# Attention on one core: which engine makes the low halves of the split scores

## The chip, the cores and the metric

The kernel runs on one core of one Trainium2 chip. The metric is the device time in microseconds (us) of one launch. Five engines work side by side and meet at semaphores: TensorE (PE in the profile, its weight loads PEld), VectorE (DVE), ScalarE (ACT), GpSimd (POOL) and SyncE (SP), which issues most of the DMAs.

## What is computed

Three layers follow each other over 16 sequences of 512 tokens with 256 features. The change lies in the second, a causal linear attention with 16 heads of 64. Cut to its core:

```python
h = _ln(x, g1, beta1)
q = _phi((h @ wq).reshape(b, s, H, DH), proj)      # phi(x) = elu(x @ proj) + 1
k = _phi((h @ wk).reshape(b, s, H, DH), proj)
v = (h @ wv).reshape(b, s, H, DH)
def step(carry, qkv_t):
    kv, ksum = carry
    kv = kv + k_t[..., :, None] * v_t[..., None, :]
    ksum = ksum + k_t
    num = jnp.einsum('bhd,bhde->bhe', q_t, kv)
    den = jnp.einsum('bhd,bhd->bh', q_t, ksum) + 1e-06
    return ((kv, ksum), num / den[..., None])
attn = moveaxis(outs) @ wo
x = x + attn
```

An MLP and a routed expert layer come behind it.

## The kernel before

The scan over tokens is done in four chunks of 128 tokens per sequence (CH = 4). Within a chunk TensorE makes the scores of key and query features, VectorE masks them, and TensorE multiplies them with the values; what lies before the chunk comes in through running sums of key times value (kvacc). All products run in float16: each operand is split into a high half (a cast) and a low half (what the cast lost), and three matmuls (high by high, low by high, high by low) give one product (the function `three`).

The 16 heads of a chunk are taken in two ways. The scores come in four quads q = 0 to 3, each a tile of 128 x 512: `scores` on TensorE writes pS, VectorE masks it into sm (L902), ScalarE casts sm to the high half sh (L796), and one engine subtracts to get the low half sl. The outputs come in four groups g = 0 to 3. Groups 0 and 1 read quads 0 and 1, groups 2 and 3 read quads 2 and 3, so `outputs` on TensorE waits for two quads when g is even (L667 to L669). Before, GpSimd makes the low halves of quads 0 and 2 (L978) and VectorE those of quads 1 and 3 (L909).

The order on every engine is written out by hand, by one function `run` that every engine walks through with its own steps. Half a sequence, a unit, is eight slots s = 0 to 7: slot s belongs to chunk 2h + s // 4 and group g = s % 4, where h is the half. In a slot an engine does, in this order: the early dense work of the table DENSE (features of the next unit "f", values "v", the projection "p"), `outputs` of this slot's group, the transposes of an earlier group, the read-out of the early dense work, `scores` of the quad that this slot brings in, `outputs_split` (on, oh, ol), the late dense work, `sums` (kvacc), `keys` (kt), `scores_split` (sh, sl), `sums_split` (kvh, kvl), a part of the split and the mixing of the input three units ahead (xh, xl), and the read-out of the late dense work (z, hi, lo). The quad of a slot runs two slots ahead of its use: slots g = 0 and 1 bring quads 2 and 3 of their own chunk, slots g = 2 and 3 bring quads 0 and 1 of the next chunk. Quad 1 is thus the last thing made before group 0 of the next chunk wants it.

I number the chunks of a sequence 1 to 4. "The outputs of chunk 2" means its group 0, which opens slot 4 of the first half, right behind slot 3, the slot of the values v0 and v1.

sm has two buffers, one for even and one for odd quads. ks, qdh and qdl (keys and queries) reach their place by DMAs of SyncE, which wait for hi and lo.

Of the kernel before, what the change touches and what calls it, by code (L numbers as in the profile page):

```python
# [10 lines left out]
ALU = mybir.AluOpType  # L11
# [13 lines left out]
CH = 4  # L25
# [29 lines left out]
def count(i, per, k):  # L55

    return i * per + k


def units(u, per, k):  # L60

    return count(u[0], 2 * per, u[1] * per + k)
# [7 lines left out]
def some(value):  # L70

    return type(value) is not int or value > 0
# [22 lines left out]
def attention_phase(nc, io, w1_w, w2_w, mlp_loaded):  # L95
# [4 lines left out]
    with ExitStack() as ctx:  # L100
        def sb(name, shape, dt=F32):
            return ctx.enter_context(nc.sbuf_tensor(name, [P, *shape], dt))

        def sem(name):
            return ctx.enter_context(nc.semaphore(name))
# [147 lines left out]
        sm = sb("sm", [2, 4, P])  # L253
        sh, sl = sb("sh", [4, 4, P], F16), sb("sl", [4, 4, P], F16)
# [22 lines left out]
            sem("qk_done"), sem("e_ready"), sem("z_read"), sem("f_ready"), sem("fh_ready"), sem("fl_ready"))  # L277
        v_done, vh_ready, vl_ready, v_ones = sem("v_done"), sem("vh_ready"), sem("vl_ready"), sem("v_ones")
        s_done, sm_ready, sh_ready = sem("s_done"), sem("sm_ready"), sem("sh_ready")
        sl_ready = [sem("sl_even"), sem("sl_odd")]  # L280
        o_done, dn_ready, rd_ready, on_ready, oh_ready, ol_ready = (
            sem("o_done"), sem("dn_ready"), sem("rd_ready"), sem("on_ready"), sem("oh_ready"), sem("ol_ready"))
        turned, turn_read = sem("turned"), sem("turn_read")
# [8 lines left out]
        def place(u):  # L292

            return (2 * u[0] + u[1]) % AHEAD
# [9 lines left out]
        def move_done(engine, w, n):  # L304


            kind = n % MOVES // 2
            engine.wait_ge(moved[kind], (128, 64)[kind] * (units(w, FEATS // MOVES, n // MOVES) + 1))
# [6 lines left out]
        def feature_back(w, n):  # L315
            return (w, n - MOVES) if n >= MOVES else (after(w, -1), n - MOVES + FEATS)

        def score_place(h):
            return 2 * (h // 8) + h % 2, (h % 8) // 2
# [227 lines left out]
        def _(pe):  # L547
            def three(out, wh, wl, mh, ml, first, last):

                pe.matmul(out, wh, mh, start=first, stop=False, skip_group_check=True)  # L550
                pe.matmul(out, wl, mh, start=False, stop=False, skip_group_check=True)  # L551
                return pe.matmul(out, wh, ml, start=False, stop=last, skip_group_check=True)  # L552
# [95 lines left out]
            def outputs(i, c, g):  # L648
                n = 4 * c + g
                toks = slice(c * P, (c + 1) * P)  # L650
                out = pO[g % 2]

                if some(count(i, 16, n - 1)):
                    pe.wait_ge(on_ready, count(i, 16, n - 1))
                first = True
                if c > 0:
                    pe.wait_ge(kvh_ready, count(i, NKV, 4 * (c - 1) + g + 1))
                    pe.wait_ge(kvl_ready, count(i, NKV, 4 * (c - 1) + g + 1))
                    for k in range(4):
                        h, part = 4 * g + k, out[:, VW * k:VW * (k + 1)]  # L660
                        pe.matmul(part, qdh[:, h, toks], kvh[:, h, :], start=first, stop=False, skip_group_check=True)
                        first = False
                        pe.matmul(part, qdh[:, h, toks], kvl[:, h, :], start=False, stop=False, skip_group_check=True)
                        pe.matmul(part, qdl[:, h, toks], kvh[:, h, :], start=False, stop=False, skip_group_check=True)
                if g % 2 == 0:

                    pe.wait_ge(sh_ready, count(i, 16, 4 * c + g + 2))  # L667
                    pe.wait_ge(sl_ready[0], count(i, 8, 2 * c + g // 2 + 1))
                    pe.wait_ge(sl_ready[1], count(i, 8, 2 * c + g // 2 + 1))  # L669
                if g == 0:  # L670
                    if type(i) is int and i == 0 and c == 0:
                        pe.wait_ge(v_ones, 2)
                    pe.wait_ge(vh_ready, count(i, 2 * VALS, 2 * c + 2))
                    pe.wait_ge(vl_ready, count(i, 2 * VALS, 2 * c + 2))
                for k in range(4):
                    h = 4 * g + k
                    q, w = score_place(h)
                    mm = three(out[:, VW * k:VW * (k + 1)], sh[:, q, w, :], sl[:, q, w, :],
                               vh[:, c, h, :], vl[:, c, h, :], first, True)
                    first = False  # L680
                mm.then_inc(o_done, 1)
# [13 lines left out]
            def turn(i, c, g):  # L695
# [6 lines left out]
                for part, src in enumerate((oh, ol)):  # L702
                    for f in range(2):
# [3 lines left out]

            run(pe, dict(mix=mix, mean=mean, var=var, features=features, values=values, scores=scores, keys=keys,
                         outputs=outputs, sums=sums, turn=turn, project=project))

        @block.scalar
# [123 lines left out]
        def _(ve):  # L835
# [60 lines left out]
            def scores(i, c, q):  # L896
                n = 4 * c + q
                ve.wait_ge(s_done, count(i, 16, n + 1))
                if some(count(i, 16, n - 1)):
                    ve.wait_ge(sh_ready, count(i, 16, n - 1))  # L900
                    ve.wait_ge(sl_ready[q % 2], count(i, 8, 2 * c + q // 2))
                nc.vector.tensor_tensor(sm[:, n % 2, :, :], pS[:, :].rearrange("p (a b) -> p a b", b=P),  # L902
                                        mask[:, :].unsqueeze(1).broadcast_to([P, 4, P]),
                                        ALU.mult).then_inc(sm_ready, 1)

            def scores_split(i, c, q):
                if q % 2 == 1:
                    ve.wait_ge(sh_ready, count(i, 16, 4 * c + q + 1))
                    nc.vector.tensor_tensor(sl[:, q, :, :], sm[:, 1, :, :], sh[:, q, :, :],  # L909
                                            ALU.subtract).then_inc(sl_ready[1], 1)  # L910

            def keys(i, c, part):
                ve.wait_ge(turned, key_turn(i, c, part))
# [43 lines left out]
        @block.gpsimd  # L957
        def _(gp):
            gp.memset(vh[:, :, :, DH:VW], 1.0).then_inc(v_ones, 1)
            gp.memset(vl[:, :, :, DH:VW], 0.0).then_inc(v_ones, 1)  # L960

            def split(u, k):
                gp.wait_ge(xh_ready, units(u, XS, k + 1))
                if some(units(u, XS, k + 1 - XS)):
                    gp.wait_ge(tok_done, units(u, XS, k + 1 - XS))
                nc.gpsimd.tensor_tensor(xl[:, k, :, :], xs[:, k, :, :], xh[:, k, :, :], ALU.subtract).then_inc(xl_ready, 1)  # L966

            def phi(w, n, bank_no):
                if units(w, FEATS, n) >= MOVES:
                    move_done(gp, *feature_back(w, n))  # L970
                gp.wait_ge(fh_ready, units(w, FEATS, n + 1))
                nc.gpsimd.tensor_tensor(lo[n % MOVES // 2][:, n % 2, :, :], z[:, units(w, FEATS, n) % ZS, :, :], hi[:, n % MOVES, :, :],  # L972
                                        ALU.subtract).then_inc(fl_ready, 1)

            def scores_split(i, c, q):
                if q % 2 == 0:
                    gp.wait_ge(sh_ready, count(i, 16, 4 * c + q + 1))
                    nc.gpsimd.tensor_tensor(sl[:, q, :, :], sm[:, 0, :, :], sh[:, q, :, :],  # L978
                                            ALU.subtract).then_inc(sl_ready[0], 1)

            def outputs_split(i, c, g):
                n = 4 * c + g
                gp.wait_ge(oh_ready, count(i, 16, n + 1))
                nc.gpsimd.tensor_tensor(ol[:, n % 2, :], on[:, n % 2, :, :].rearrange("p a b -> p (a b)"),  # L984
                                        oh[:, n % 2, :], ALU.subtract).then_inc(ol_ready, 1)

            def sums_split(i, c, g):
                u = 4 * c + g
                gp.wait_ge(kvh_ready, count(i, NKV, u + 1))
                heads = slice(4 * g, 4 * g + 4)  # L990
                nc.gpsimd.tensor_tensor(kvl[:, heads, :], kvacc[:, heads, :], kvh[:, heads, :],  # L991
                                        ALU.subtract).then_inc(kvl_ready, 1)

            def residual(u):
                gp.wait_ge(x1_ready, units(u, 1, 1))
                gp.wait_ge(h_ready, units(u, 1, 1))
                gp.wait_ge(hb_ready, units(u, DT, DT))
                nc.gpsimd.tensor_tensor(hT[:, place(u), :, :], hT[:, place(u), :, :], x0[:, place(u), :, :],
                                        ALU.add).then_inc(hx_ready, 1)

            run(gp, dict(residual=residual, split=split, phi=phi, scores_split=scores_split, outputs_split=outputs_split,
                         sums_split=sums_split))

# [1194 lines left out]
```

## Time and profile before

| what | value |
|---|---|
| median of 3 runs | 2622.9 us (2621.56 to 2630.17) |
| profiled execution, its time | 2629.9 us |
| profiled execution, its span | 2628.2 us |
| PE busy | 2258.0 us, 86% |
| DVE busy | 1783.4 us, 68% |
| ACT busy | 1525.8 us, 58% |
| POOL busy | 1468.2 us, 56% |
| attention, from its first outputs to its last | about 113 to 1525 us of the span |

Busy time is a share of the whole span, in which three stages follow each other; only the attention stage holds the instructions that the change moves. One sequence takes 90 us there. A busy PE is one whose matmul records overlap, so a stall shows as an idle time in front of a matmul, in square brackets in the timeline.

### The profile page before, as it was taken

The page shows a single profiled execution, that of the slowest core. Times are in us where ns is not written, and L with a number is a line of the kernel's source. Part 1 is how long each engine was busy: PE and PEld are TensorE (multiplying, and loading weights), DVE is VectorE, ACT ScalarE, POOL GpSimd, SP SyncE. Part 2 cuts the span into 40 slices and gives each one's busy share as a digit, 9 for nine tenths or more (in the row PEclk, how much of TensorE's full clock was granted, in tenths as well). Part 3 has the DMA queues.
Part 4 walks back from the last instruction along what each step waited for, and adds up shares of the span by engine and source line. Part 5 has one row for each costly group of instructions (what it writes and reads, how often), then busy time and mean ns, then how long its engine had stood idle before and what let it go on. Part 6 is the DMA issues. An engine that isn't in the chain of part 4 may idle for free. (4 is left out here: it accounts for less than half of the span.)

```text
span 2628.2 us, 64033 instructions
## 1 busy us (share of the span) xinstructions
PE 2258.0 (86%) x24112; PEld 1738.2 (66%) x24112; DVE 1783.4 (68%) x3983; ACT 1525.8 (58%) x2890; POOL 1468.2 (56%) x1449
## 2 busy tenths in 40 slices
PE   3799999999999999999999858989998999894774
PEld 2588787878787887878787736555555555552553
DVE  2477778777777777777777746766776677664442
ACT  3576777767777777677677645544554455441232
POOL 1376666666666756666666621553454345436576
PEclk8899999999999999999999979999999999997887
DMA  3344444444444434444443330111111111000775
GB/s 109 101 129 126 108 123 128 123 117 123 125 116 123 115 97 114 100 105 105 114 102 90 82 107 33 57 52 54 42 57 66 40 35 46 27 21 17 156 141 71
DMA packets 310913, 236.32 MB, mean 90 GB/s; under 512 B 28057, under 2 KB 275853, under 8 KB 310608
## 3 DMA queue, kind: packets, MB, share of 16 engines
q1 hardware_dynamic: 274352, 197.25, 28.1%
q0 software_dynamic: 23808, 21.74, 4.7%
q10 hardware_dynamic: 12448, 13.24, 1.6%
q8 instruction: 194, 3.18, 0.5%
q14 instruction: 111, 0.91, 0.1%
HBM read 73.32 MB, written 82.58 MB: 59 GB/s over the span
## 5 line engine op out<-in xcount | busy, mean ns | idle before, releaser
L1857 POOL DMA_INDIRECT slot_dram<-xt,slot_u x256 | 267.4, 1045 | 77.1 <-issue 77.1
L550 PE MATMUL pF<-nh,qk_h 128*128 128x256 f16 x1024 | 281.7, 275 | 7.8 <-DVE nl L869 4.4
L551 PE MATMUL pF<-nh,qk_l 128*128 128x256 f16 x1024 | 281.5, 275 | 0.0
L552 PE MATMUL pF<-nl,qk_h 128*128 128x256 f16 x1024 | 281.3, 275 | 0.0
L972 POOL TENSOR_TENSOR lo<-z,hi 128x512 f16<-128x512 f32 x128 | 148.6, 1161 | 198.6 <-DVE hi L881 198.6
L1845 POOL TENSOR_TENSOR xt<-xn,xt 128x512 f16<-128x512 f32 x32 | 40.0, 1269 | 330.5 <-ACT xt L1528 330.5
L796 ACT ACTIVATE sh<-sm 128x512 f16<-128x512 f32 x256 | 160.0, 625 | 88.2 <-DVE sm L902 82.5
L984 POOL TENSOR_TENSOR ol<-on,oh 128x256 f16<-128x256 f32 x256 | 172.2, 673 | 69.5 <-ACT oh L819 69.5
L876 DVE SCALAR_TENSOR_TENSOR z<-pF,z 128x512 f32<-128x512 f32 x256 | 175.1, 684 | 41.6 <-ACT z L779 39.0
L972 POOL TENSOR_TENSOR w_w<-z,hi 128x512 f16<-128x512 f32 x128 | 157.7, 1232 | 60.4 <-DVE hi L881 60.4
L991 POOL TENSOR_TENSOR kvl<-kvacc,kvh 128x260 f16<-128x260 f32 x192 | 157.9, 822 | 50.3 <-ACT kvh L827 50.3
L902 DVE TENSOR_TENSOR sm<-pS,mask 128x512 f32<-128x512 f32 x256 | 174.4, 681 | 10.1 <-PE pS L636 10.1
L1309 PE MATMUL pY<-w_h,gh 128*128 128x256 f16 x512 | 154.5, 302 | 30.0 <-issue 29.8
L550 PE MATMUL pO<-vh,sh 128*128 128x65 f16 x1024 | 119.4, 193 | 67.7 <-issue 48.1
L881 DVE CAST hi<-z 128x512 f16<-128x512 f32 x256 | 170.5, 666 | 8.8
L775 ACT ACTIVATE z<-pF 128x512 f32<-128x512 f32 x256 | 149.9, 586 | 45.1 <-PE pF L552 42.9
L966 POOL TENSOR_TENSOR xl<-w_w,xh 128x512 f16<-128x512 f32 x128 | 148.0, 1159 | 47.3 <-ACT xh L726 47.3
L1311 PE MATMUL pY<-w_l,gh 128*128 128x256 f16 x512 | 154.1, 301 | 22.4 <-issue 22.0
L1310 PE MATMUL pY<-w_h,gl 128*128 128x256 f16 x512 | 154.6, 302 | 18.6 <-issue 18.4
L803 ACT ACTIVATE ot<-pT 128x512 f16<-128x512 f16 x256 | 149.8, 585 | 31.0 <-PE pT L705 30.3
L779 ACT ACTIVATE z<-z 128x512 f32<-128x512 f32 x256 | 161.3, 630 | 8.2
L2107 POOL DMA_INDIRECT out_rows<-yb,xg x80 | 126.7, 1584 | 61.4 <-ACT yb L2052 35.9
(299 smaller groups left out, 8517.1 us busy)
## 6 DMA issues: line engine op xcount, KB each, us to landing
w_w<-in_x SPq DMA_DIRECT2D x128, 256.0 KB, 3.0
qdh<-hi SPq DMA_DIRECT2D x256, 128.0 KB, 2.7
qdl<-lo SPq DMA_DIRECT2D x256, 128.0 KB, 2.8
ks<-hi SPq DMA_DIRECT2D x128, 128.0 KB, 3.1
ks<-w_w SPq DMA_DIRECT2D x128, 128.0 KB, 3.1
slot_dram<-blank ACTq DMA_DIRECT2D x8, 1360.0 KB, 6.7
xg<-slot_dram SPq DMA_DIRECT2D x40, 272.0 KB, 2.9
x_dram<-x SPq DMA_DIRECT2D x32, 256.0 KB, 2.2
```

The lines of the kernel that those rows point to most:

```text
L550: pe.matmul(out, wh, mh, start=first, stop=False, skip_group_check=True)
L551: pe.matmul(out, wl, mh, start=False, stop=False, skip_group_check=True)
L552: return pe.matmul(out, wh, ml, start=False, stop=last, skip_group_check=True)
L779: nc.scalar.activation(z[:, s, :, :], z[:, s, :, :], ACT.Exp, scale=-1.0, bias=-math.log(PHI_DOWN)).then_inc(e_ready, 1)
L796: nc.scalar.activation(sh[:, q, :, :], sm[:, n % 2, :, :], ACT.Copy).then_inc(sh_ready, 1)
L876: nc.vector.scalar_tensor_tensor(z[:, s, :, :], pF[bank_no][:, :].rearrange("p (b n) -> p b n", b=2), 0.0, z[:, s, :, :], ALU.max, ALU.add ...
L881: nc.vector.tensor_copy(hi[:, n % MOVES, :, :], z[:, s, :, :]).then_inc(fh_ready, 1)
L902: nc.vector.tensor_tensor(sm[:, n % 2, :, :], pS[:, :].rearrange("p (a b) -> p a b", b=P), mask[:, :].unsqueeze(1).broadcast_to([P, 4, P]) ...
L972: nc.gpsimd.tensor_tensor(lo[n % MOVES // 2][:, n % 2, :, :], z[:, units(w, FEATS, n) % ZS, :, :], hi[:, n % MOVES, :, :], ALU.subtract).t ...
L984: nc.gpsimd.tensor_tensor(ol[:, n % 2, :], on[:, n % 2, :, :].rearrange("p a b -> p (a b)"), oh[:, n % 2, :], ALU.subtract).then_inc(ol_re ...
L991: nc.gpsimd.tensor_tensor(kvl[:, heads, :], kvacc[:, heads, :], kvh[:, heads, :], ALU.subtract).then_inc(kvl_ready, 1)
L1857: nc.gpsimd.indirect_dma_start(io["slot_dram"], bass.IndirectOffsetOnAxis(slot_u[:, i % XT, c, k:k + 1], 0), xt[:, i % XT, c, :], None, bo ...
```

## The change

The low halves of quads 0 and 1 change engines: GpSimd now makes those of quads 1 and 2, VectorE those of quads 0 and 3. Each engine still makes two of four. The semaphore that counted the low halves by parity becomes one for each quad, and every wait keeps its meaning. In the slots this means that the subtraction of slots 2 and 6 (quad 0) moves from GpSimd to VectorE and that of slots 3 and 7 (quad 1) from VectorE to GpSimd.

```diff
-        sl_ready = [sem("sl_even"), sem("sl_odd")]
+        sl_ready = [sem(f"sl_ready{q}") for q in range(4)]
...
-                    pe.wait_ge(sl_ready[0], count(i, 8, 2 * c + g // 2 + 1))
-                    pe.wait_ge(sl_ready[1], count(i, 8, 2 * c + g // 2 + 1))
+                    pe.wait_ge(sl_ready[g], count(i, CH, c + 1))
+                    pe.wait_ge(sl_ready[g + 1], count(i, CH, c + 1))
...
-                    ve.wait_ge(sl_ready[q % 2], count(i, 8, 2 * c + q // 2))
+                    ve.wait_ge(sl_ready[(q + 2) % 4], count(i, CH, c + q // 2))
...
             def scores_split(i, c, q):
-                if q % 2 == 1:
+                if q in (0, 3):
                     ve.wait_ge(sh_ready, count(i, 16, 4 * c + q + 1))
-                    nc.vector.tensor_tensor(sl[:, q, :, :], sm[:, 1, :, :], sh[:, q, :, :],
-                                            ALU.subtract).then_inc(sl_ready[1], 1)
+                    nc.vector.tensor_tensor(sl[:, q, :, :], sm[:, q % 2, :, :], sh[:, q, :, :],
+                                            ALU.subtract).then_inc(sl_ready[q], 1)
...
             def scores_split(i, c, q):
-                if q % 2 == 0:
+                if q in (1, 2):
                     gp.wait_ge(sh_ready, count(i, 16, 4 * c + q + 1))
-                    nc.gpsimd.tensor_tensor(sl[:, q, :, :], sm[:, 0, :, :], sh[:, q, :, :],
-                                            ALU.subtract).then_inc(sl_ready[0], 1)
+                    nc.gpsimd.tensor_tensor(sl[:, q, :, :], sm[:, q % 2, :, :], sh[:, q, :, :],
+                                            ALU.subtract).then_inc(sl_ready[q], 1)
```

On VectorE, in slots 2 and 3 of the first half, from the transposed keys kt of slot 2 to the first instruction of the outputs of chunk 2 (dn), the order before is:

```order
L917 COPY kt<-pT 128x1024
L876 SCALAR_TENSOR_TENSOR z<-pF,z 128x512
L881 CAST hi<-z 128x512
L886 SCALAR_TENSOR_TENSOR vl<-pF,vh 128x8x64
L926 TENSOR_SCALAR dn<-pO 128x4
L929 RECIPROCAL rd<-dn 128x4
L934 TENSOR_TENSOR on<-pO,rd 128x256
L902 TENSOR_TENSOR sm<-pS,mask 128x512
L886 SCALAR_TENSOR_TENSOR vl<-pF,vh 128x8x64
L947 COPY kvacc<-pKV 128x260
L909 TENSOR_TENSOR sl<-sm,sh 128x512
L926 TENSOR_SCALAR dn<-pO 128x4
```

The same stretch of VectorE with the change:

```order
L917 COPY kt<-pT 128x1024
L909 TENSOR_TENSOR sl<-sm,sh 128x512
L876 SCALAR_TENSOR_TENSOR z<-pF,z 128x512
L881 CAST hi<-z 128x512
L886 SCALAR_TENSOR_TENSOR vl<-pF,vh 128x8x64
L926 TENSOR_SCALAR dn<-pO 128x4
L929 RECIPROCAL rd<-dn 128x4
L934 TENSOR_TENSOR on<-pO,rd 128x256
L902 TENSOR_TENSOR sm<-pS,mask 128x512
L886 SCALAR_TENSOR_TENSOR vl<-pF,vh 128x8x64
L947 COPY kvacc<-pKV 128x260
L926 TENSOR_SCALAR dn<-pO 128x4
```

The subtraction stood last, behind the mask of quad 1 (sm) that it needs; now one stands ahead of z, and the mask of quad 1 comes after it. On GpSimd, in the same two slots, from the residual (hT) of slot 2 to the input split (xl) of slot 3, the order before is:

```order
L998 TENSOR_TENSOR hT<-hT,x 128x512
L984 TENSOR_TENSOR ol<-on,oh 128x256
L978 TENSOR_TENSOR sl<-sm,sh 128x512
L991 TENSOR_TENSOR kvl<-kvacc,kvh 128x260
L966 TENSOR_TENSOR xl<-w_w,xh 128x512
L972 TENSOR_TENSOR w_w<-z,hi 128x512
L984 TENSOR_TENSOR ol<-on,oh 128x256
L991 TENSOR_TENSOR kvl<-kvacc,kvh 128x260
L966 TENSOR_TENSOR xl<-w_w,xh 128x512
```

And with the change (w_w at L972 is the low half of key features, lo):

```order
L998 TENSOR_TENSOR hT<-hT,x 128x512
L984 TENSOR_TENSOR ol<-on,oh 128x256
L991 TENSOR_TENSOR kvl<-kvacc,kvh 128x260
L966 TENSOR_TENSOR xl<-w_w,xh 128x512
L972 TENSOR_TENSOR w_w<-z,hi 128x512
L984 TENSOR_TENSOR ol<-on,oh 128x256
L978 TENSOR_TENSOR sl<-sm,sh 128x512
L991 TENSOR_TENSOR kvl<-kvacc,kvh 128x260
L966 TENSOR_TENSOR xl<-w_w,xh 128x512
```

GpSimd's subtraction moves five places back, behind the ol of slot 3. TensorE, ScalarE and SyncE keep their order.

## Rows read from the trace of the kernel before

**Rows 1.** Windows, most of the attention stage: length, busy time and instructions by engine, PEclk, DMA

```profile
150.00:1450.00 1300.00, 1213.44 (x16192) 1040.27 (x16190) 1004.52 (x2081) 922.77 (x1875) 851.32 (x893) 1.00 0.44 114
```

**Rows 2.** Waits of PE from 150 to 1450: us in total, times, longest

```profile
PE pO L550 <- issue: 44.5, 29, 1.8
PE pT L645 <- ACT ot L803: 31.2, 28, 1.5
PE pO L550 <- DVE sl L909: 8.9, 28, 0.7
```

**Rows 3.** Timeline, chunk 1 of a sequence: start, length, instruction, idle before it

```profile
1011.11 0.42 ACT L819 ACTIVATE oh<-on 128x256 f16<-128x256 f32 x1 [0.55 <-DVE on L934]
...
1011.60 0.68 POOL L984 TENSOR_TENSOR ol<-on,oh 128x256 f16<-128x256 f32 x1 [1.97 <-ACT oh L819]
...
1011.70 0.63 ACT L796 ACTIVATE sh<-sm 128x512 f16<-128x512 f32 x1 [0.18 <-DVE sm L902]
...
1012.36 0.69 DVE L909 TENSOR_TENSOR sl<-sm,sh 128x512 f16<-128x512 f32 x1 [0.70 <-ACT sh L796]
...
1013.42 0.19 PE L550 MATMUL pO<-vh,sh 128*128 128x65 f16 x1 [0.43 <-DVE sl L909]
```

**Rows 4.** Timeline, chunk 2: PE, its features f4 and its outputs

```profile
1034.31 0.28 PE L550 MATMUL pF<-nh,qk_h 128*128 128x256 f16 x1
...
1037.97 0.19 PE L550 MATMUL pO<-vh,sh 128*128 128x65 f16 x1 [1.81 <-issue]
```

**Rows 5.** Timeline, slots 2 and 3 ahead of chunk 2: DVE

```profile
1031.12 0.68 DVE L917 COPY kt<-pT 128x1024 f16<-128x1024 f16 x1
...
1032.43 1.23 DVE L881 CAST hi<-z 128x512 f16<-128x512 f32 x1
1033.57 0.68 DVE L886 SCALAR_TENSOR_TENSOR vl<-pF,vh 128x512 f16<-128x512 f32 x1
...
1036.90 0.68 DVE L909 TENSOR_TENSOR sl<-sm,sh 128x512 f16<-128x512 f32 x1
```

**Rows 6.** Timeline, chunk 3: DVE's subtraction, and the outputs on PE

```profile
1057.43 0.69 DVE L909 TENSOR_TENSOR sl<-sm,sh 128x512 f16<-128x512 f32 x1 [0.36 <-ACT sh L796]
...
1058.50 0.19 PE L550 MATMUL pO<-vh,sh 128*128 128x65 f16 x1
```

**Rows 7.** Timeline, slots 2 and 3 again: POOL, and ACT's cast of quad 1

```profile
1031.58 0.68 POOL L984 TENSOR_TENSOR ol<-on,oh 128x256 f16<-128x256 f32 x1
1032.21 1.16 POOL L978 TENSOR_TENSOR sl<-sm,sh 128x512 f16<-128x512 f32 x1
...
1034.15 1.15 POOL L966 TENSOR_TENSOR xl<-w_w,xh 128x512 f16<-128x512 f32 x1
...
1035.83 0.62 ACT L796 ACTIVATE sh<-sm 128x512 f16<-128x512 f32 x1
```

**Rows 8.** Timeline, DVE and POOL in each other's way, and a cast left alone

```profile
1002.51 0.67 POOL L984 TENSOR_TENSOR ol<-on,oh 128x256 f16<-128x256 f32 x1
1003.13 1.13 POOL L991 TENSOR_TENSOR kvl<-kvacc,kvh 128x260 f16<-128x260 f32 x1
...
1002.54 1.18 DVE L909 TENSOR_TENSOR sl<-sm,sh 128x512 f16<-128x512 f32 x1 [0.36 <-ACT sh L796]
...
1004.36 0.43 DVE L881 CAST hi<-z 128x512 f16<-128x512 f32 x1
```

**Rows 9.** Timeline, the end of the stage: PE released by POOL

```profile
1514.47 0.69 POOL L991 TENSOR_TENSOR kvl<-kvacc,kvh 128x260 f16<-128x260 f32 x1
...
1515.31 0.19 PE L661 MATMUL pO<-kvh,qdh 128*128 128x65 f16 x1 [1.21 <-POOL kvl L991]
```

**Rows 10.** Timeline, slot 7 of the second half: DVE waits for the values

```profile
1009.64 0.69 DVE L886 SCALAR_TENSOR_TENSOR vl<-pF,vh 128x512 f16<-128x512 f32 x1 [1.84 <-ACT vh L785]
```

**Rows 11.** Timeline, in the opening of the stage: a long wait of PE

```profile
85.20 1.40 PE L579 MATMUL pM<-w_w,ones 128*128 128x256 f32 x4 [2.93 <-ACT w_w L737]
```

**Rows 12.** Windows, behind that wait, columns as in rows 1

```profile
85.90:89.30 3.40, 3.40 (x16) 2.22 (x16) 1.15 (x3) 2.05 (x5) 0.00 (x0) 0.50 0.00 0
```

## The prediction

> **What bounds the kernel now.** I read the windows first: over 1300 us of attention PE is busy 1213, VectorE 1005, ScalarE 923, GpSimd 851 [rows 1]. TensorE bounds the stage, and only what makes it stand still counts. The waits of PE say where that is: 85 us in all, and 53 of them stand in front of the first matmul that uses sh and sl, pO at L550 [rows 2]. So the change touches the largest stall there is. 44.5 us of it carry the label "issue", which names nobody, so I went to the timeline. In each sequence there are four such places, the outputs of chunks 1 to 4, and they differ.
>
> Chunk 1: the high half of quad 1 ends at 1012.33, VectorE's subtraction runs 1012.36 to 1013.05, TensorE starts at 1013.42 after 0.43 us idle [rows 3]. The subtraction is the last link. Chunk 2: the subtraction ends at 1037.58 and TensorE starts 0.39 later, having stood for 1.81 [rows 4, 5]; the 29 "issue" waits, two in each sequence, have a mean of 44.5 / 29 = 1.53 [rows 2], so chunks 2 and 4 are alike: the subtraction releases TensorE there too. Chunk 3: it ends at 1058.12, TensorE comes at 1058.50 without idle time [rows 6]. In chunk 1 TensorE needed 0.37 from that end, where a bare wait takes 0.06 [rows 4, 5], so its slack here lies between 0 and 0.32; I take 0.17, the middle.
>
> In slots 2 and 3 ahead of chunk 2 VectorE is the one who is late: its cast hi takes 1.23 instead of 0.43, because GpSimd's sl runs from 1032.21 to 1033.37, and the cast ends 0.29 behind it [rows 5, 7, 8].
>
> **The change part by part.** Each engine keeps two of four subtractions, so busy times hardly move. What moves is who stands last, and what is in front.
>
> *Quad 1 from VectorE to GpSimd, all four places.* GpSimd takes 1.16 [rows 7] where VectorE takes 0.69: +0.47. It starts 0.07 to 0.08 behind ScalarE (oh ends at 1011.53, ol starts at 1011.60 [rows 3]), VectorE 0.03: +0.05. Its queue is clear: ol ends at 1012.28, before sh does [rows 3]. TensorE starts 0.15 behind the end of a GpSimd instruction (1515.16 to 1515.31 [rows 9]); behind VectorE it takes 0.06 where one wait is all (vl ends 1034.25, f4 starts 1034.31 [rows 4, 5]): +0.09. Together 0.61. Chunk 1 pays all of it. Chunk 3 pays 0.61 - 0.17 = 0.44.
>
> *Quad 0 from GpSimd to VectorE, slots 6.* VectorE then waits for the values v3, 1.84 us [rows 10]. A subtraction of 0.7 to 1.2 fits under this wait: nothing. If that cover were gone, it would cost these.
>
> *Quad 0 from GpSimd to VectorE, slots 2.* Here VectorE has no gap. kt ends at 1031.80 [rows 5], the high half of quad 0 is ready then, and sl would start at 1031.82. But GpSimd's ol runs until 1032.26 [rows 7]. The same pair meets in another slot [rows 8]: VectorE's sl begins 0.03 behind the start of ol, lasts 1.18 instead of 0.69 and ends 0.54 behind the end of ol, and GpSimd's next, kvl, ends 0.54 behind sl instead of taking its usual 0.68. So sl ends near 1032.80, a full microsecond behind kt. The cast starts 0.63 behind the end of what stands ahead of z (kt 1031.80, hi 1032.43 [rows 5]): 1033.43. GpSimd now has kvl, then xl: kvl ends at 1033.34, xl starts 0.04 before that, at 1033.30, and takes 1.15 [rows 7], to 1034.45. The cast comes 0.13 too late, waits, and ends 0.29 behind xl at 1034.74, against 1033.66 now. So v0's low half, on, oh, the mask of quad 1 and its high half all come 1.08 later; VectorE works through them without a pause worth counting. GpSimd has caught up by then (lo, then ol, end before sh, at 1036.45 + 1.08 = 1037.53 [rows 7]).
>
> From the end of sh to the end of sl it is now 1037.58 - 1036.45 = 1.13, as kvacc stands in the way; on GpSimd 0.08 + 1.16 = 1.24: +0.11. With the reaction of 0.09 and the 1.08 this is 1.28 in chunk 2, and the same in chunk 4, whose slots hold the same instructions. I take the whole 1.08 because both meetings are of a kind that the trace shows. Its ends are 0.22 if the cast gets in ahead of xl, when GpSimd's delayed queue makes the sum some 0.41; and some 1.5 if GpSimd's next instruction also got in ahead of sl. Part of this stall shows earlier: f4 waits for v0's low half and starts 0.06 behind it [rows 4, 5], so about 1 us of idle time appears in front of pF.
>
> *Sum.* 0.61 + 1.28 + 0.44 + 1.28 = 3.61 us for a sequence. The first and the last sequence lack a part, so 15.5 of them: **+56 us**. The profiled time is 2629.9, within 0.3% of the median of 2622.9; the same increment on the median gives **2679**. The delays are not made good elsewhere, since all the chains behind start from TensorE.
>
> The Trainium skill (GPSIMD Engine Reference, Instruction dispatch) puts the floor of a two-input GpSimd operation at about 2.5 cycles per element. At its 1.2 GHz that is an estimate of 1.07 us for 512 elements; with it the four places would cost 0.36 less in a sequence, and the sum would be some 50 us. The rows have 1.16, and I go by them.
>
> **The rivals.** *The cast is not caught (0.12).* The margin is 0.13 us, the difference of sums over several rows. If hi starts before xl, chunks 2 and 4 pay 0.41 each: 0.61 + 0.44 + 0.82 = 1.87, times 15.5 is 29, so 2652. For it: the margin is small. Against it: nothing in front of xl waits. The Trainium skill (SBUF — State Buffer, Who interferes with whom) says that the first of the two to start holds the shared ports for its whole instruction, the other blocks; by that rule the cast loses, with xl started 0.13 before it.
>
> *The clock (0.06).* In the opening TensorE stood 2.93 us [rows 11], and from 85.90 to 89.30 its granted clock was 0.50, the lower level of 1.2 GHz [rows 12]; in attention it is 1.00 with stalls up to 1.81 [rows 1, 4]. The longer stall is parted by f4 into about 1.0 and 1.75, so I expect no fall. If each of 31 places fell for 3.4 us, half of that is lost: 31 x 1.7 = 53 more, 2732.
>
> *Absorbed (0.05).* TensorE also waits for ot, 31.2 / 28 = 1.11 each, twice in a sequence [rows 2]. Were that set by a chain that does not start from the delayed TensorE, 2.2 of 3.61 would vanish: 1.4 x 15.5 = 22, so 2645. That chain starts with the mean and the variance that TensorE makes in slots 0 and 1, so I doubt it.
>
> *Faster (0.04).* The "issue" stalls could hang on GpSimd's queue, which is relieved of 1.16 in slots 2. Then chunks 2 and 4 gain up to 1.16 each, against 0.61 + 0.44: 1.27 x 15.5 = 20, so 2603. It decides once they gain over 0.53 each. Against it: in chunk 1 the trace names sl at L909 as the releaser, and in chunk 2 TensorE starts just as long behind it, 0.39 and 0.37 [rows 3, 4, 5].
>
> *No change (0.05).* If the "issue" stalls hang on neither, only chunk 1's 0.61 stays: 15 x 0.61 = 9, at the edge of what can be told from nothing. About 0.3% either way, 8 us, is what this kernel's measurement can tell.
>
> **The numbers.** The forecast has 0.68. The range goes from 2645, which takes in the absorbed and the uncaught case, to 2698, which takes in double waits at the ports and a few falls of the clock; it leaves out the two cases of no loss and most of the clock's. Slower by over 0.3% are the forecast, the uncaught cast, the absorbed case and the clock: 0.91. Same 0.05, faster 0.04.
>
> **What would show it.** sl at L978 stays near 1.16 and now releases pO; it ends 1.24 behind the end of sh. sl at L909 in slots 2 lasts about 1.0, and hi behind it about 1.3. PE shows new idle time before pF in slot 4 (about 1 us, less in the second half) 1.0 instead of 0.4 in chunk 1, a short one in chunk 3. Wrong would be: hi at 0.43 in slots 2, a shorter stall at chunk 2, or PEclk under 1.00.

## The result and the profile after

The changed kernel took 2678.8 us (median of 4 runs, 2675.07 to 2681.81), the kernel before 2622.85 (4 runs, 2621.56 to 2630.17). The ratio is 1.0207, 95% interval 1.0184 to 1.023. The profiled execution after took 2675.07 us, its span is 2673.3. The change costs 2%, as forecast.

The page of after, its busy times, and under them the window that answers to [rows 1]:

```profile
PE 2265.6 (85%) x24112; PEld 1738.0 (65%) x24112; DVE 1799.2 (67%) x3983; ACT 1529.3 (57%) x2890; POOL 1484.3 (56%) x1449
...
150.00:1450.00 1300.00, 1182.46 (x15618) 1005.67 (x15616) 988.06 (x2007) 895.57 (x1813) 839.94 (x865) 1.00 0.43 111
```

The granted clock in this window is 1.00 as before; in the same 1300 us TensorE is busy 31 us less. The waits of PE from 150 to 1450, against [rows 2]:

```profile
PE pO L550 <- issue: 50.7, 42, 1.7
PE pT L645 <- ACT ot L803: 31.0, 28, 1.5
PE pO L550 <- POOL sl L978: 13.0, 14, 0.9
PE pF L550 <- DVE z L876: 12.6, 28, 0.6
PE pF L550 <- DVE vl L886: 6.3, 28, 0.2
PE pO L550 <- DVE sl L909: 2.3, 14, 0.2
```

The stall in front of the first outputs, named after DVE's sl before, is now named after GpSimd's and is twice as long (13.0 / 14 = 0.93). "issue" has 42 waits, three in each sequence: chunk 3 has joined. Two waits in front of pF are new.

A stage of 16 like sequences is best compared by its period. I took the start of the first pO<-vh,sh matmul of each chunk from the timeline; means over sequences 2 to 15, in us (the 15th has less work ahead of it and shorter intervals, in every kernel alike):

| interval | before | after | difference | forecast |
|---|---|---|---|---|
| outputs of chunk 1 to 2 | 24.45 | 25.59 | +1.14 | +1.28 |
| chunk 2 to 3 | 20.53 | 20.87 | +0.34 | +0.44 |
| chunk 3 to 4 | 25.34 | 26.42 | +1.08 | +1.28 |
| chunk 4 to 1 of the next | 19.58 | 20.08 | +0.51 | +0.61 |
| period | 89.90 | 92.96 | +3.06 | +3.61 |

From the first outputs of the stage to the last it is 1411.1 us before and 1460.8 after: +49.7.

Slots 2 and 3 ahead of chunk 2, the timeline of after, beside [rows 4, 5, 7] (the same sequence, some 31 us later in the span):

```profile
1061.90 0.68 DVE L917 COPY kt<-pT 128x1024 f16<-128x1024 f16 x1
...
1062.36 0.67 POOL L984 TENSOR_TENSOR ol<-on,oh 128x256 f16<-128x256 f32 x1
...
1062.60 0.98 DVE L909 TENSOR_TENSOR sl<-sm,sh 128x512 f16<-128x512 f32 x1
...
1062.99 1.13 POOL L991 TENSOR_TENSOR kvl<-kvacc,kvh 128x260 f16<-128x260 f32 x1
...
1064.08 1.15 POOL L966 TENSOR_TENSOR xl<-w_w,xh 128x512 f16<-128x512 f32 x1
...
1064.21 1.30 DVE L881 CAST hi<-z 128x512 f16<-128x512 f32 x1
...
1064.23 0.39 PE L550 MATMUL pF<-wv_h,nh 128*128 128x512 f16 x1 [0.63 <-DVE z L876]
...
1066.17 0.28 PE L550 MATMUL pF<-nh,qk_h 128*128 128x256 f16 x1 [0.23 <-DVE vl L886]
...
1067.68 0.62 ACT L796 ACTIVATE sh<-sm 128x512 f16<-128x512 f32 x1
...
1068.38 1.15 POOL L978 TENSOR_TENSOR sl<-sm,sh 128x512 f16<-128x512 f32 x1 [0.34 <-ACT sh L796]
...
1069.75 0.19 PE L550 MATMUL pO<-vh,sh 128*128 128x65 f16 x1 [1.72 <-issue]
```

VectorE's sl starts behind kt inside GpSimd's ol, lasts 0.98 and ends a microsecond behind kt. xl starts 0.13 ahead of the cast hi, which lasts 1.30 and ends 0.28 behind xl. Both meetings are there, and even the margin of 0.13 is the one that the prediction gave. At the end ACT's sh ends at 1068.30, GpSimd's sl 1.23 later at 1069.53, and TensorE starts 0.22 behind it.

### The profile page after: what moved, and what is told of

It is laid out like the page before. It is cut to its first block and busy times, and to the rows that moved or that the text cites. A ratio compares the mean times of both kernels' runs of the same rounds, so it can differ in the third digit from the quotient of the medians.

```text
span 2673.3 us, 64033 instructions
## 1 busy us (share of the span) xinstructions
PE 2265.6 (85%) x24112; PEld 1738.0 (65%) x24112; DVE 1799.2 (67%) x3983; ACT 1529.3 (57%) x2890; POOL 1484.3 (56%) x1449
## 5 line engine op out<-in xcount | busy, mean ns | idle before, releaser
L972 POOL TENSOR_TENSOR lo<-z,hi 128x512 f16<-128x512 f32 x128 | 148.5, 1160 | 179.7 <-DVE hi L881 179.7
L972 POOL TENSOR_TENSOR w_w<-z,hi 128x512 f16<-128x512 f32 x128 | 157.6, 1231 | 73.1 <-DVE hi L881 73.1
L991 POOL TENSOR_TENSOR kvl<-kvacc,kvh 128x260 f16<-128x260 f32 x192 | 170.6, 889 | 32.6 <-ACT kvh L827 32.4
L926 DVE TENSOR_SCALAR dn<-pO 128x4 f32<-128x4 f32 x256 | 40.1, 157 | 192.3 <-PE pO L552 191.9
L819 ACT ACTIVATE oh<-on 128x256 f16<-128x256 f32 x256 | 105.7, 413 | 105.8 <-DVE on L934 101.6
```

## The experiments

Each kernel was timed beside the kernel before on the same chip. Several chips were used, and they differ by up to 5% for the same kernel (last section); so only increments over the kernel before count, and they are made from the median and from the period. Intervals as in the table above, in us.

| run | before, same chip | median | ratio (95%) | 1 to 2 | 2 to 3 | 3 to 4 | 4 to 1 | period |
|---|---|---|---|---|---|---|---|---|
| e1 slots 6, 7 only | 2501.11 | 2520.19 | 1.0064 (1.005 to 1.0078) | 24.44 | 20.88 | 25.34 | 20.11 | 90.77 |
| e2 slots 2, 3 only | 2501.11 | 2539.54 | 1.0149 (1.0134 to 1.0165) | 25.60 | 20.53 | 26.43 | 19.55 | 92.11 |
| e3 VectorE makes three | 2501.11 | 2534.2 | 1.0125 (1.011 to 1.0141) | 25.50 | 20.54 | 26.31 | 19.61 | 91.95 |
| e4 GpSimd makes three | 2501.11 | 2540.8 | 1.0157 (1.014 to 1.0174) | 24.97 | 21.00 | 25.83 | 20.41 | 92.21 |
| e5 lo ahead of xl | 2610.99 | 2641.42 | 1.0106 (1.0087 to 1.0125) | 24.89 | 20.88 | 25.74 | 20.10 | 91.61 |
| e6 sl ahead of kvacc | 2610.99 | 2636.78 | 1.0095 (1.0078 to 1.0113) | 24.44 | 21.40 | 25.31 | 20.50 | 91.65 |
| e7 kvl ahead of sl | 2610.99 | 2609.67 | 0.9995 (0.9984 to 1.0005) | 24.44 | 20.53 | 25.31 | 19.56 | 89.84 |
| e8 lo right behind ol | 2610.99 | 2607.05 | 0.9984 (0.9975 to 0.9994) | 24.42 | 20.53 | 25.28 | 19.56 | 89.78 |
| e9 and xl of slots 2 later | 2625.73 | 2623.63 | 0.9997 (0.9987 to 1.0007) | 24.01 | 20.88 | 24.89 | 19.98 | 89.75 |
| e10 semaphores only | 2625.73 | 2626.3 | 1.0004 (0.9995 to 1.0014) | | | | | 89.88 |
| e11 and xl of slots 4 later | 2610.06 | 2901.37 | 1.1117 (1.1102 to 1.1133) | 33.55 | 20.66 | 35.82 | 19.45 | 109.49 |
| e12 and its load later | 2502.17 | 2494.02 | 0.9963 (0.9949 to 0.9976) | 24.20 | 20.67 | 24.88 | 19.46 | 89.22 |

### e10: the semaphores alone

The four semaphores of the change, with the engines of before. In it and in all other runs the engine is picked by one function:

```diff
+        def on_vector(c, q):
+            return q % 2 == 1
...
-                if q in (0, 3):
+                if on_vector(c, q):
...
-                if q in (1, 2):
+                if not on_vector(c, q):
```

> Edit: only the four semaphores of the change; engines and order as before. Both theories: no change, the period of a sequence stays at 89.90 us. It is also the profile of the kernel before's work on this chip.

The ratio holds 1, the period is that of before. All of the 56 us comes from the exchange of engines.

### e1 and e2: the exchange in two halves

c counts the chunks from 0, so an even c is chunk 1 or 3, made in slots 6 and 7.

```diff
-            return q % 2 == 1
+            return q in (0, 3) if c % 2 == 0 else q % 2 == 1     # e1
+            return q in (0, 3) if c % 2 == 1 else q % 2 == 1     # e2
```

> Edit: the exchange is made only for the quads of chunks 1 and 3 (slots 6 and 7); chunks 2 and 4 keep the engines of before. My theory (the last link is slower by about 0.5 us, and VectorE's extra subtraction in slots 6 lies under its wait for v3): the stall before the outputs of chunk 1 goes from 0.43 to 0.93 us, chunk 3 gets one of 0.18, chunks 2 and 4 stay at 1.66 and 1.42; period of a sequence +0.85 us, so about +13 us, some 2636 us on 2623. Rival (each moved subtraction costs the same wherever it stands, so half of the loss is here): about +28 us, 2651.

> Edit: the exchange is made only for the quads of chunks 2 and 4 (slots 2 and 3). My theory: all that the full change lost beyond chunks 1 and 3 is here, as VectorE has no gap in slots 2, its subtraction waits out ol (about 0.98 us) and its cast waits out xl (1.30 instead of 1.23): period +2.2 us, so +34 us, some 2657. The outputs of chunks 1 and 3 have stalls of 0.43 and 0 as before. Rival (even shares): +28 us, 2651. Rival (the parts are not additive, one hides the other): e1 and this one do not add up to the +56 us of the whole.

Each half moves its own intervals and no other, by the amounts of the full change to 0.03 us. Over the stage they cost 16.4 and 34.1 us, together 50.5, against 49.7 for the whole. The price splits by place as the prediction had it: two thirds at slots 2 and 3. Nothing is made good elsewhere, and the granted clock from 150 to 1450 is 1.00 in both.

### e3 and e4: one direction at a time

```diff
-            return q in (0, 3)
+            return q != 2      # e3: VectorE quads 0, 1, 3
+            return q == 3      # e4: GpSimd quads 0, 1, 2
```

> Edit: VectorE makes the low halves of quads 0, 1 and 3, GpSimd that of quad 2 alone. Quad 1 is VectorE's as before, only quad 0 is added to it. My theory (half of the loss is VectorE's lateness in slots 2, which does not depend on who is last): chunks 1 and 3 as before, chunks 2 and 4 about 1.05 us later each, period +2.1 us, +33 us, some 2656. Rival (the whole loss is GpSimd as the last link, with the same subtraction 0.47 us longer at four places): nothing lost, 2623, since VectorE is last here again.

e3 moves quad 0 to VectorE and leaves quad 1 there: chunks 1 and 3 are free (19.61 and 20.54), chunks 2 and 4 pay 1.05 and 0.97. That is the VectorE lateness alone, where I had 1.08, and it is nine tenths of what these chunks pay in the full change.

> Edit: GpSimd makes the low halves of quads 0, 1 and 2, VectorE that of quad 3 alone. Now VectorE is relieved and only the last link is moved. My theory: chunks 1 and 3 lose 0.51 and 0.34 us as in the full change; in chunks 2 and 4 VectorE's cast is as late as before, but GpSimd still has lo and ol in front (ol ends at 1037.04 in the trace of before, where the high half is there at 1036.45), so its subtraction ends about 0.58 later than VectorE's did: period +2.0 us, +31 us, some 2654. Rival (GpSimd's queue is clear there too, as with the full change): chunks 2 and 4 lose only 0.07 to 0.11 each, period +1.0 us, +16 us, 2639. Rival (last link is all of the loss): the full +56 us, 2679.

e4 moves quad 1 to GpSimd and leaves quad 0 there. Chunks 2 and 4 lose 0.52 and 0.49; chunks 1 and 3 lose 0.83 and 0.47, more than in the full change (0.51 and 0.34). The excess is TensorE's clock. The stalls ahead of chunks 2 and 4 are 2.21 and 1.97 here, and behind five of these 28 the granted clock fell to 0.50 for 3.4 us. One stall of e4, and the windows of the stage and of the fall behind that stall:

```profile
967.05 0.19 PE L553 MATMUL pO<-vh,sh 128*128 128x65 f16 x1 [2.21 <-issue]
```

```profile
150.00:1450.00 1300.00, 1192.22 (x15755) 1019.60 (x15753) 936.79 (x1969) 906.64 (x1826) 889.70 (x929) 0.99 0.43 112
968.50:971.90 3.40, 3.40 (x18) 2.42 (x17) 1.91 (x4) 1.86 (x4) 2.34 (x4) 0.50 0.34 86
```

Four of the falls make an interval from chunk 4 to 1 longer by 1.3 us, one makes an interval from chunk 2 to 3 longer by 1.7. In the inner sequences that no fall touches, these intervals are 20.2 and 20.9, as in the full change. Without the five falls e4 costs 0.52, 0.35, 0.49 and 0.46, together 1.82, near the 2.0 that I expected. e3 and e4 together (2.05 + 1.82) are still more than the exchange (3.06). The difference lies in chunks 2 and 4: with quad 0 left on GpSimd, quad 1 costs them 0.52 and 0.49 there; with quad 0 gone (after against e3) only 0.09 and 0.11.

### e5: the cast let through

The full change, and in slots 2 GpSimd makes v0's low half lo ahead of its step of the input split, so that it waits for the cast instead of standing in its way.

```diff
+                    lo_first = "lo_before_split" in steps and s == 2
+                    if lo_first:
+                        for what in late:
+                            finish(u, *what[:2])
...
                         step("split", far, s - 1)
...
-                    for what in late:
+                    for what in late if not lo_first else ():
```

> Edit: the full change, and in slots 2 GpSimd makes lo (the low half of the features) ahead of xl, so that after kvl it stands waiting for VectorE's cast instead of working beside it. My theory (the cast waits out xl): the cast takes 0.43 instead of 1.30, the masks and high halves of quad 1 come 0.87 earlier, GpSimd's subtraction, now behind xl and ol, some 0.77 earlier in chunks 2 and 4: period 1.5 us shorter than with the full change, so +32 us on the kernel before instead of +56. Rival (VectorE's lateness is just its one more subtraction and no lock): the cast stays long whatever GpSimd does, +56 us, or GpSimd's later xl makes it worse.

Timeline of e5, the cast in slots 2:

```profile
1033.43 0.43 DVE L888 CAST hi<-z 128x512 f16<-128x512 f32 x1
```

It takes 0.43 instead of 1.30. Chunks 2 and 4 fall from 25.59 and 26.42 to 24.89 and 25.74, 0.70 and 0.68 less; slots 6 and 7 are untouched. This is the uncaught cast of my first rival, built: 24.89 - 24.45 = +0.44, where I had worked out 0.41. The capture of the cast by xl is shown to be the cause of 0.7 of the 1.1. The cast itself gives back 0.87; GpSimd, which makes xl later, then ends its subtraction 1.37 behind sh instead of 1.23. The period is 1.35 shorter than with the full change (expected 1.5), and the median is 30 us above the kernel before (expected 32).

### e6: can the old order be improved by starting sl earlier?

The engines of before; in slots 3 VectorE makes sl ahead of kvacc.

```diff
+                    halves_first = "halves_before_sums" in steps and s == 3 and quad is not None
+                    if halves_first:
+                        step("scores_split", *quad)
                     if summed is not None:
                         step("sums", i, *summed)
...
-                    if quad is not None:
+                    if quad is not None and not halves_first:
```

> Edit: engines of before; in slots 3 VectorE makes the low half of quad 1 ahead of kvacc instead of behind it. My theory (that subtraction is the last link to the outputs of chunks 2 and 4): it starts 0.33 us earlier, both stalls shrink by 0.33, period -0.66 us, -10 us in all. Rival (kvacc is later by as much, ScalarE's kvh waits for it and holds up the features behind it): nothing gained or a loss.

The rival was right: a loss. Timeline of e6, and below it one of the waits of PE from 150 to 1450:

```profile
1053.24 1.03 DVE L915 TENSOR_TENSOR sl<-sm,sh 128x512 f16<-128x512 f32 x1
...
1054.64 0.42 ACT L833 ACTIVATE kvh<-kvacc 128x260 f16<-128x260 f32 x1 [1.53 <-DVE kvacc L953]
...
1056.76 0.69 DVE L882 SCALAR_TENSOR_TENSOR z<-pF,z 128x512 f32<-128x512 f32 x1 [0.89 <-ACT z L785]
```

```profile
PE pO L556 <- DVE sl L915: 26.9, 42, 1.2
```

sl starts earlier, but inside GpSimd's ol, lasts 1.03 instead of 0.69 and ends no sooner (1.15 behind sh, as before). kvacc behind it is late; ScalarE stands 1.53 for it at kvh and makes the features z behind that, so VectorE's z stands 0.89. The third group of outputs then waits for VectorE's low half of quad 3: the waits for DVE's sl are 26.9 us in 42, against 8.9 in 28 before. The period grows by 1.75.

### e7, e8, e9: taking the cast out of GpSimd's way before

If GpSimd's sl costs 0.8 us of cast in the kernel before, moving it should gain. All three keep the engines of before. In e7 GpSimd makes kvl ahead of sl in slots 2 and 6; in e8 its order in slots 2 is ol, lo, kvl, sl, xl; e9 is e8 with the xl of slot 2 moved behind ol and kvl of slot 3.

```diff
+                    kvl_first = "kvl_before_halves" in steps and g == 2      # e7
+                    if summed is not None and kvl_first:
+                        step("sums_split", i, *summed)
...
+                    lo_first = "lo_first" in steps and s == 2                # e8, e9
+                    if lo_first:
+                        for what in late:
+                            finish(u, *what[:2])
+                        step("sums_split", i, *summed)
...
+                    if "lo_first" in steps and s == 3 and real(far):         # e9
+                        step("split", far, 1)
...
-                    if 1 <= s <= XS and real(far):
+                    if 1 <= s <= XS and real(far) and not lo_first:          # e9
```

What is made early is left out at its old place, in lines not shown here.

> Edit: engines of before; in slots 2 and 6 GpSimd makes kvl (0.68 us) ahead of the low half of quad 0 (1.16 us). My theory (VectorE's cast in slots 2 waits for whatever GpSimd has begun): it waits for the shorter one, ends 0.48 us earlier, and so does the subtraction of quad 1: period -0.96 us, -15 us. Rival (the chain to the outputs of chunks 2 and 4 does not run through that cast): 0.

> Edit: engines of before; in slots 2 GpSimd makes lo right behind ol, then kvl, then the low half of quad 0, then xl. GpSimd idles beside the cast. My theory: the cast takes 0.43 instead of 1.23, all behind it on VectorE comes 0.80 earlier, stalls before the outputs of chunks 2 and 4 from 1.66 and 1.42 to about 0.9 and 0.6: period -1.6 us, -25 us. Rival (GpSimd, pushed back by about 0.8, makes quad 0's low half or kvl the last one): the stalls are released by GpSimd and less is gained, or nothing.

Neither gained what it freed. Timeline of e8, the subtraction that releases TensorE, and GpSimd beside it:

```profile
1034.94 1.15 POOL L974 TENSOR_TENSOR xl<-w_w,xh 128x512 f16<-128x512 f32 x1
...
1035.55 1.09 DVE L917 TENSOR_TENSOR sl<-sm,sh 128x512 f16<-128x512 f32 x1
```

The cast was at 0.43, everything behind it came earlier, and then sl(q1) met xl and waited it out (1.09 for 0.68). In e7 it met ol in the same way (1.12). The time freed at one meeting was taken by the next.

> Edit: the kernel with lo right behind ol in slots 2 and the engines of before, and there GpSimd's xl of slot 2 moves behind the ol and kvl of slot 3, so that GpSimd waits idle at kvl while VectorE subtracts for quad 1. In the last trace VectorE's subtraction stood from 1035.55 until xl ended (1036.09) and ended 0.55 behind it, at 1036.64. My theory (this lock took back what the earlier cast had won): ol now comes right behind the low half of quad 0 and ends near 1035.6, the subtraction 0.55 behind it at 1036.2, chunks 2 and 4 gain 0.4 to 0.5 each on that kernel, period -0.9 us, -14 us, and some -18 us on the kernel before. Rival (the stall hangs on something else that I have not seen): again no gain at chunks 2 and 4.

Timeline of e9, the same subtraction, and below it the waits of PE from 150 to 1450:

```profile
1035.29 0.68 DVE L919 TENSOR_TENSOR sl<-sm,sh 128x512 f16<-128x512 f32 x1
```

```profile
PE pO L560 <- issue: 33.2, 29, 1.4
...
PE pO L560 <- DVE sl L919: 17.5, 41, 0.7
```

Now sl is free and chunks 2 and 4 gain 0.44 and 0.45 over before. But the 28 waits for DVE's sl of [rows 2] are 41: the later intervals lose 0.35 and 0.40, and the period is 0.15 below before. No measurable gain in the median (0.9997, expected some -18 us).

### e11 and e12: out of slots 4 too

In e9 GpSimd makes two xl one behind the other in slots 3, and they run into slots 4, where they catch VectorE's first cast. Timeline of e9:

```profile
1036.54 2.28 POOL L976 TENSOR_TENSOR xl<-w_w,xh 128x512 f16<-128x512 f32 x2
...
1038.25 0.85 DVE L891 CAST hi<-z 128x512 f16<-128x512 f32 x1
```

It takes 0.85 where it took 0.43 before. The cast of slots 5, which the expectation of e11 names, takes 1.09 before too, so it is not what e9 added; it is one more meeting that can be cleared. e11 is e9 with GpSimd's xl of slots 4 moved to slots 6; e12 moves SyncE's load of that part as well. The lines are those of e12; e11 asks for `lo_first` at both places, which only GpSimd has.

```diff
+                    if "xl_late" in steps and s == 6 and real(far):
+                        step("split", far, 3)
-                    if 1 <= s <= XS and real(far) and not lo_first:
+                    if 1 <= s <= XS and real(far) and not lo_first and not ("xl_late" in steps and s == 4):
                         step("split", far, s - 1)
...
-            run(sp, dict(split=split, phi=phi, residual=residual))
+            run(sp, dict(xl_late=True, split=split, phi=phi, residual=residual))     # e12 only
```

> Edit: the last version (lo right behind ol in slots 2, its xl behind kvl in slots 3, engines of before) and GpSimd's xl of slots 4 moved to slots 6, where GpSimd has idle time. There the 0.44 us won at chunks 2 and 4 came back as 0.35 and 0.43 us of stall before the third group of outputs of the same chunks, behind a cast in slots 5 that waits out that xl (1.10 instead of 0.43). My theory: the cast in slots 5 takes 0.43, the subtraction of quad 3 comes 0.66 earlier, the won time is kept: period about -0.85 us, -13 us, a version about 0.5% faster than the kernel before. Rival (SyncE waits for that xl before its next load and holds up the moves of keys and queries behind it, or the mixing waits for xl): given back again, or a loss.

The rival won by far: +11%. Waits of PE and of SP's queue in e11, from 150 to 1450, and its window:

```profile
PE pS L647 <- issue: 217.1, 24, 12.6
...
SPq L498 <- POOL xl L978: 445.2, 59, 12.3
```

```profile
150.00:1450.00 1300.00, 1035.73 (x13023) 875.18 (x13021) 792.87 (x1673) 740.11 (x1510) 686.64 (x723) 0.90 0.38 95
```

SyncE's load of the next part waits for xl to release the buffer (up to 12.3 us, against 5.5 before), and the DMAs that bring ks, qdh and qdl stand behind it in SyncE's queue. So a late xl became late keys and queries: 217 us of TensorE in front of the scores, 9.0 at a time. The granted clock is 0.90 here, in a window where e4 has 0.99 and every other kernel 1.00; these stalls reach 12.6 us, where those of e4 reach 2.2 and those of the others 1.8.

> Edit: the last version, and SyncE's load of that part of the input also moves from slots 4 to 6, behind the moves of the last features. In the last trace SyncE stood up to 12.3 us at that load (L498) until xl was made, and the keys and queries queued behind it came that much later, which TensorE paid with 7.7 and 9.1 us before its scores. My theory: with the load moved along nothing waits behind it, the loss goes, and what was expected of the last version shows: cast in slots 5 at 0.43, no stall before the third group of outputs, period about -0.85 us on the kernel before, -13 us. Rival (the loss did not hang on SyncE's queue but on xl itself, late for the mixing): still a loss of many us.

With the load moved too the queue is clear. Waits of PE in e12:

```profile
PE pO L562 <- issue: 33.4, 29, 1.5
...
PE pM L562 <- POOL xl L978: 7.5, 14, 0.5
...
PE pO L562 <- DVE sl L921: 1.2, 1, 1.2
```

The waits for DVE's sl at chunk 1 are gone but for one; a wait for xl of 0.5 has come in front of the mixing. The period is 89.22, 0.66 below the semaphores alone, and the median 2494.02 against 2502.17: 0.4% faster than the kernel before, 8 us where I expected 13. That is the best version found. It keeps the engines of before.

## Why the prediction was right, and where its terms were off

*The bound, and the four places.* Right. TensorE bounds the stage, nothing downstream gave the delay back (e1 and e2 add up to the whole), and the granted clock was 1.00 from 150 to 1450.

*Quad 0 to VectorE in slots 2.* Right in mechanism and nearly in size. e3 measures the lateness at 1.05 and 0.97 (forecast 1.08), and e5 shows that 0.7 of it is the cast behind xl. sl lasted 0.98 and hi 1.30. The rule of the Trainium skill (SBUF — State Buffer, Who interferes with whom), that the first to start holds the shared ports and the other blocks, agrees: xl started 0.13 ahead of hi, and hi ended 0.28 behind it. The first rival, which came to +29 us, needed hi to get in ahead, and it did not.

*Quad 0 to VectorE in slots 6.* Right: e3 leaves the intervals that end at chunks 1 and 3 alone, to 0.03.

*Quad 1 to GpSimd.* The longer operation and its slower start are as forecast (sl ends 1.23 behind sh, forecast 1.24). The floor that I had worked out from the Trainium skill (GPSIMD Engine Reference, Instruction dispatch), an estimate of 1.07, stays below every one measured, 1.15 to 1.18. The term of 0.09 for TensorE's reaction was mis-sized: it is nothing. Timeline of after, chunk 1 and chunk 3:

```profile
1042.69 1.15 POOL L978 TENSOR_TENSOR sl<-sm,sh 128x512 f16<-128x512 f32 x1
...
1044.20 0.19 PE L550 MATMUL pO<-vh,sh 128*128 128x65 f16 x1 [0.93 <-POOL sl L978]
...
1089.24 1.16 POOL L978 TENSOR_TENSOR sl<-sm,sh 128x512 f16<-128x512 f32 x1
...
1090.62 0.19 PE L550 MATMUL pO<-vh,sh 128*128 128x65 f16 x1 [0.18 <-issue]
```

In chunk 1 TensorE starts 0.36 behind GpSimd's sl; behind VectorE's it was 0.37 [rows 3]. In chunks 2 and 4 it is 0.21 behind GpSimd's sl, and before it was 0.21 behind VectorE's too. The place that I had read, with 0.39 and a stall of 1.81 [rows 4, 5], is an odd one. Timeline of before, chunk 2 of another sequence:

```profile
1127.06 0.69 DVE L909 TENSOR_TENSOR sl<-sm,sh 128x512 f16<-128x512 f32 x1
...
1127.96 0.19 PE L550 MATMUL pO<-vh,sh 128*128 128x65 f16 x1 [1.65 <-issue]
```

I had compared one bare wait on each engine; here several waits stand ahead of the matmul, and the releaser's engine does not show. Without the four times 0.09 the sum is 3.25 for a sequence, and 3.06 was measured. The slack of chunk 3, guessed at 0.17 from bounds of 0 and 0.32, is that: TensorE came 0.38 behind sl before, without a wait [rows 6], and comes 0.22 behind it where it waits. The interval lost 0.34, and 0.52 less 0.17 is 0.35.

*The clock.* I expected no fall, and from 150 to 1450 of the full change there is none, with stalls up to 1.73. It was nearer than I thought: in e4 stalls of 1.97 and 2.21 were enough for five falls. I had priced one at 1.7; they cost 1.3 to 1.7. In the last sequence the full change has two falls that the kernel before has not (see the sum).

*Where the lateness shows.* Partly wrong. I expected about 1 us in front of f4. f4 shows 0.23, and v1 ahead of it, which waits for VectorE's read-out z of the bank, 0.63; I had not looked at what of z TensorE waits for. The sum in front of pF is 0.86. The rest does not appear as idle time at all. Windows over 13 whole sequences, before and after:

```profile
204.32:1373.02 1168.70, 1090.50 (x14530) 934.68 (x14528) 903.67 (x1868) 829.77 (x1686) 769.76 (x806) 1.00 0.45 115
```

```profile
207.56:1416.04 1208.48, 1100.20 (x14531) 935.62 (x14528) 920.37 (x1868) 832.82 (x1686) 782.94 (x806) 1.00 0.43 112
```

The same matmuls are busy 9.7 us longer, 0.75 a sequence; idle time grew by (1208.48 - 1100.20) - (1168.70 - 1090.50) = 30.1 us, of 39.8 in all. The profile's busy time counts overlapping records once, so a matmul that runs out alone ahead of a new stall adds to it. That reading is argued, not tested; the numbers say that a quarter of the loss is in no square bracket.

*The sum.* That 2679 met the median to 0.2 us is luck: the errors offset each other. The period was forecast 0.55 too high. Against that, 14 inner sequences at 3.06 make 42.8 of the 49.7 that the stage lost, so the first and the last lose 6.9 together where I had counted 1.5 periods, 4.6 at the measured price. Most of the excess is the clock in the last sequence. Its stalls ahead of chunks 1 and 3 grew by about 1.1 each (1.79 to 2.91, 1.77 to 2.83), and the clock fell behind both, where before it fell behind neither. Windows of after:

```profile
1507.70:1511.10 3.40, 3.40 (x29) 2.66 (x27) 2.03 (x4) 1.93 (x4) 1.79 (x3) 0.50 0.02 5
1548.60:1552.00 3.40, 3.40 (x54) 3.40 (x52) 2.18 (x7) 2.63 (x6) 2.35 (x3) 0.50 0.02 5
```

In the last sequence the intervals from chunk 1 to 2 and from 3 to 4, in which these falls lie, are 22.35 and 18.50; in e2, which makes the same exchange for chunks 2 and 4 and has no fall there, they are 21.44 and 17.52. So the two falls cost about 0.9 and 1.0. And the profiled executions differ by 45.1 us of span where the medians differ by 56: the one of before lay 7 above its median, that of after 4 below. Worked from the stage, the increment is 50; the remaining 6 are within what runs of one kernel differ by (2621.56 to 2630.17), and the interval of the ratio allows 48 to 60.

## What to carry to other kernels

When two engines share work evenly, ask not who does how much but who does the piece that is made last before the bounding engine waits: the slower engine there costs its difference (0.5 in chunk 1), and little where the faster one was held up anyway (0.1 in chunks 2 and 4, behind kvacc). Then follow the neighbours of every moved instruction in time, since VectorE and GpSimd wait out each other's operations and a microsecond freed at one meeting is easily taken by the next (e7, e8); to gain, clear all meetings up to the release, and move the loads that share the buffer along with them (e11, e12). Judge such a change by the period of a repeating stage: it was 89.90 and 89.88 in before and e10, and intervals that e1, e2 and e3 left alone kept to 0.03 on the chip that is 5% faster. Look at the single sequences behind a mean, too, and at the granted clock beside each: e4's falls hid in its mean.

## What the runs showed of the hardware

*Meetings of VectorE and GpSimd.* A cast that takes 0.43 alone and starts 0.10 to 0.80 into a GpSimd operation ends 0.28 behind that one's end; VectorE's sl, 0.69 alone, ends 0.55 behind it. Begun in about the last 0.15 us of the GpSimd operation, sl is not lengthened. A kvl or ol of GpSimd that waits behind VectorE's sl then ends 0.53 to 0.54 behind it.

*The clock in attention.* From 150 to 1450 the granted clock fell behind no stall of up to 1.83 us in any kernel but e11; in e4 it fell behind five of 28 stalls of 1.97 or 2.21; in e11, with stalls up to 12.6, its mean is 0.90.

*The clock outside attention.* The stage repeats (89.90 and 89.88), but what comes behind it took 1081 to 1104 us on some chips and 976 to 979 on another. Windows of the MLP, 1630 to 2250, in before and in e12:

```profile
1630.00:2250.00 620.00, 558.78 (x3750) 345.11 (x3748) 423.58 (x1088) 314.62 (x489) 293.06 (x264) 0.93 0.15 50
```

```profile
1630.00:2250.00 620.00, 617.34 (x4546) 403.43 (x4543) 505.71 (x1310) 369.69 (x574) 348.27 (x314) 1.00 0.16 53
```

On the one chip the clock fell once in every MLP iteration, on the other not at all, and 4546 matmuls were done in the time of 3750. It goes with the chip and not with the change: e1, too, has 1.00 there, on the chip that ran the kernel before in 2501.11 us; after, on a chip with falls, has 0.93. What causes it was not tested and stays open.
